# One-core macaron block (MoE, attention, MoE): the down products alternate between two PSUM banks, and the attention's products share the two that are left

## What is computed

```python
x = x + 0.5 * ffn(layernorm(x))          # first pass  (a = 0)
x = x + attention(layernorm(x))
x = x + 0.5 * ffn(layernorm(x))          # second pass (a = 1), the same weights

def ffn(x):                               # 2048 tokens of width 256, 8 experts of width 512
    w = top_p_weights(softmax(x @ router_w.T), 0.9)
    for e in range(8):
        out += (silu(x @ gate_w[e].T) * (x @ up_w[e].T)) @ down_w[e].T * w[:, e:e + 1]

def attention(x):                         # 8 sequences of 256; 16 query heads, 4 KV heads, width 16
    q, k, v = rope(rms_norm(x @ Wq.T + bq)), rope(rms_norm(x @ Wk.T + bk)), x @ Wv.T + bv
    return softmax(causal(q @ k.T / 4)) @ v @ Wo.T + bo
```

## Time and profile before

| what | value |
|---|---|
| three runs | 1108.98 us median, 1108.06 to 1111.28 |
| the profiled execution | 1108.69 us, span of the core 1107.0 us |
| PE matmuls busy | 1087.7 us, 98% of the span |
| DVE / ACT / POOL busy | 853.8 / 546.2 / 641.0 us |
| mean granted TensorE clock | 0.996 |

### The profile page before, as it was taken

One profiled execution on the slowest core, in us unless ns is written; L12 is line 12 of the kernel. 1 busy time (PEld: TensorE's weight loads), 2 busy tenths in 40 slices (PEclk: granted clock), 3 DMA queues, 4 the chain that ended last, 5 costly groups with the idle time before them and its releaser, 6 DMA issues.

```text
span 1107.0 us, 21233 instructions
## 1 busy us (share of the span) xinstructions
PE 1087.7 (98%) x7624; PEld 657.0 (59%) x7624; DVE 853.8 (77%) x1810; ACT 546.2 (49%) x1027; POOL 641.0 (58%) x673
## 2 busy tenths in 40 slices
PE   6899999999999999999999999999999999999998
PEld 4466656565665655566566566656656566666655
DVE  7988788767878887889888789888888765644443
ACT  4545554333555655645655555555555553333332
POOL 4545343346668677778677678586686643322332
PEclk8999999999999999999999999999999999999999
DMA  5311120010133333323333523443243320000000
GB/s 191 127 58 57 58 82 1 1 25 20 35 67 63 61 60 68 58 49 67 65 56 53 86 41 61 74 84 61 49 68 59 78 57 6 6 20 1 1 1 20
DMA packets 166008, 57.96 MB, mean 52 GB/s; under 512 B 158096, under 2 KB 162704, under 8 KB 165904
## 3 DMA queue, kind: packets, MB, share of 16 engines
q1 hardware_dynamic: 165904, 56.61, 24.7%
HBM read 15.70 MB, written 2.10 MB: 16 GB/s over the span
## 4 chain that ended last, share of the span: by engine, by line
PE 79%; DVE 3%; POOL 3%; issue 1%; DMA 1%; ACT 0%; DVEq 0%; ACTq 0%; POOLq 0%; SPq 0%
PE YB L358 25%; PE G L339 25%; PE U L339 24%; PE S L448 2%; PE S L431 1%; PE S L413 1%; PE S L459 1%; POOL room L1090 1%; POOL HS L1006 1%; DMA QKT<-room 1%; DVE TS L625 0%; DVE X L646 0%; ACT TS L500 0%; POOL RR L1063 0%; PE S L358 0%
## 5 line engine op out<-in xcount | busy, mean ns | idle before, releaser
L1006 POOL TENSOR_TENSOR HS<-TS,HS 128x512 f16<-128x512 f32 x256 | 300.7, 1176 | 394.8 <-ACT HS L507 394.1
L358 PE MATMUL YB<-W,HS 128*128 128x256 f16 x3036 | 373.4, 273 | 7.0 <-DVE X L646 4.6
L339 PE MATMUL G<-XS,W 128*128 128x512 f16 x1536 | 374.7, 380 | 0.3 <-ACT XS L533 0.3
L339 PE MATMUL U<-XS,W 128*128 128x512 f16 x1536 | 373.5, 379 | 0.0
L358 PEld LDWEIGHTS YB<-W,HS 128*128 128x128 f16 x3036 | 292.0, 98 | 89.4 <-DVE X L646 8.8
L507 ACT ACTIVATE HS<-TS 128x512 f16<-128x512 f32 x256 | 161.0, 629 | 320.5 <-DVE TS L630 319.3
L625 DVE SCALAR_TENSOR_TENSOR TS<-TS,G 128x512 f32<-128x512 f32 x256 | 174.8, 683 | 136.8 <-ACT TS L500 134.9
L500 ACT ACTIVATE TS<-G,TSC 128x512 f32<-128x512 f32 x256 | 175.1, 684 | 189.6 <-PE G L339 186.5
L339 PEld LDWEIGHTS U<-XS,W 128*128 128x128 f16 x1536 | 150.4, 98 | 181.7 <-issue 0.8
L339 PEld LDWEIGHTS G<-XS,W 128*128 128x128 f16 x1536 | 146.2, 98 | 131.9 <-issue 4.1
L630 DVE SCALAR_TENSOR_TENSOR TS<-TS,U 128x512 f32<-128x512 f32 x256 | 175.9, 687 | 27.8 <-DVE TS L625 0.5
(11 more groups left out here) (168 smaller groups left out, 759.1 us busy)
## 6 DMA issues: line engine op xcount, KB each, us to landing
room<-in_gate SPq DMA_DIRECT2D x4, 512.0 KB, 4.0
room<-in_up SPq DMA_DIRECT2D x4, 512.0 KB, 4.0
room<-in_down SPq DMA_DIRECT2D x4, 512.0 KB, 3.9
QKT<-in_gate SPq DMA_DIRECT2D x4, 512.0 KB, 4.8
QKT<-in_up SPq DMA_DIRECT2D x4, 512.0 KB, 4.0
QKT<-in_down SPq DMA_DIRECT2D x4, 512.0 KB, 4.7
out_y<-X SPq DMA_DIRECT2D x16, 128.0 KB, 1.8
X<-in_x SPq DMA_DIRECT2D x3, 512.0 KB, 6.9
```

The costliest lines, as they stand in the source:

```text
L339: mm = eng.matmul(bank[:, :], W[:, e, wl, jj, kk * I + m * P:kk * I + (m + 1) * P], flat(XS16[:, b % 2, xl, kk, :, :], 'cq'), start=q == 0 ...
L358: mm = eng.matmul(out, HS[:, j % 2, hl, kk, m * P:(m + 1) * P], W[:, e, wl, 2, kk * D:(kk + 1) * D], start=kk + hl + wl == 0, stop=kk == K ...
L1006: eng.tensor_tensor(HS[:, j % 2, 1, m, :], TS[:, k % 3, :], HS[:, j % 2, 0, m, :], ALU.subtract).then_inc(L['g_lo'].sem, 1)
```

## The change

Down products with odd `k` from `Y2` = 9 on go to `S2`, the others stay in `YB`, so `pe_y(k)` waits for the reading of `k-2` in place of `k-1`. PV moves to `S0`, and Q/K/V, projection and all logits to `S1`; `s2_read` goes, and its waits are split between `s0_read` and `s1_read`, which the scores ask too. The tables of slots are written anew, and the start of the lists of PE, ACT, DVE and POOL is reordered.

```diff
+Y2 = 9
-ROUND_AT = (2, 8, 13, 19, 27, 32)
+ROUND_AT = (2, 7, 14, 20, 26, 32)
-FTP0 = (0, 1, 2, 2)
+FTP0 = (0, 0, 2, 3)
-EVEN_STEP = {'ma': 1, 'mb': 2, 'ea': 3, 'eb': 3, 'ha': 5, 'hb': 5, 'la': 4, 'lb': 4, 't': 2, 'pv': 8, 'o': 8}
-ODD_STEP = {'ma': 1, 'mb': 2, 'ea': 2, 'eb': 3, 'ha': 2, 'hb': 4, 'la': 3, 'lb': 4, 't': 3, 'pv': 8, 'o': 9}
+EVEN_STEP = {'ma': 1, 'mb': 2, 'ea': 3, 'eb': 4, 'ha': 5, 'hb': 5, 'la': 4, 'lb': 4, 't': 3, 'pv': 10, 'o': 11}
+ODD_STEP = {'ma': 1, 'mb': 2, 'ea': 2, 'eb': 3, 'ha': 3, 'hb': 5, 'la': 3, 'lb': 4, 't': 4, 'pv': 8, 'o': 10}
-W_FIRST = {'mx': 0, 'wt': 3, 'wr': 3, 'wb': 5, 'sc': 5, 'hi': 7, 'lo': 7}
-ATT, QKVP, OUTP = (by_tile(-24, -12), by_tile(-11, 1), by_tile(18, 42))
+W_FIRST = {'mx': 1, 'wt': 3, 'wr': 2, 'wb': 4, 'sc': 5, 'hi': 7, 'lo': 7}
+ATT, QKVP, OUTP = (by_tile(-24, -12), by_tile(-12, 0), by_tile(25, 43))
...
+        def y_bank(k):
+            return S2 if k >= Y2 and k % 2 else YB
+
         def logits(r):
-            return (S1 if r < 3 else S2)[:, 0:BT * 3 * E]
+            return S1[:, 0:BT * 3 * E]
...
         def s0_read(eng, s):
             eng.wait_ge(*L['a_e'].at(before(ROUND, s), 'a'))
+            eng.wait_ge(*L['v_pv'].at(before(AT['pv'], s), 'rd'))
...
         def s1_read(eng, s):
             eng.wait_ge(*L['a_e'].at(before(ROUND, s), 'b'))
-            eng.wait_ge(*L['v_ls'].at(before(ROUTE[:3], s), 'ls'))
+            eng.wait_ge(*L['v_ls'].at(before(ROUTE, s), 'ls'))
+            eng.wait_ge(*L['v_qb'].at(before(QKVP, s), 'qb'))
+            eng.wait_ge(*L['v_op'].at(before(OUTP, s, O_STEP['mm']), 'ad'))
...
             if bank is None:
-                bank = YB
-                eng.wait_ge(*L['v_y'].at(k - 1, 'y'))
+                bank = y_bank(k)
+                eng.wait_ge(*L['v_y'].at(k - 1 if y_bank(k - 1) is bank else k - 2, 'y'))
+                if k == Y2:
+                    eng.wait_ge(*L['a_fc'].at(2 * BT - 1, 'xs'))
...
         def pe_pv(eng, i, s):
             t, j = ROUNDS[i]
-            s2_read(eng, s)
+            s0_read(eng, s)
...
-                    o = S2[:, n * VW:(n + 1) * VW]
+                    o = S0[:, n * VW:(n + 1) * VW]
...
             act_fc(eng, 1)
-            act_w(eng, 0, 0)
             act_fx(eng, 2)
             act_fx(eng, 3)
+            act_fc(eng, 2)
+            act_w(eng, 0, 0)
             act_w(eng, 0, 1)
-            act_fc(eng, 2)
             act_fc(eng, 3)
```

More of the change, by code:

```diff
@@ L310, in s1_read @@
                 eng.wait_ge(*L['v_wq'].at(0, 'cl'))
-        def s2_read(eng, s):
-            eng.wait_ge(*L['v_pv'].at(before(AT['pv'], s), 'rd'))
-            eng.wait_ge(*L['v_qb'].at(before(QKVP, s), 'qb'))
-            eng.wait_ge(*L['v_op'].at(before(OUTP, s, O_STEP['mm']), 'ad'))
-            f = max((f for f in range(1, 2 * BT, 2) if FTP[f] < s), default=-1)
-            eng.wait_ge(*L['a_fc'].at(f, 'xs'))
-            if before(ROUTE, s) >= 3:
-                eng.wait_ge(*L['v_ls'].at(before(ROUTE, s), 'ls'))
         def pe_warm(eng, n):
@@ L383, in pe_lg @@
         def pe_lg(eng, r, s):
-            (s1_read if r < 3 else s2_read)(eng, s)
+            s1_read(eng, s)
             if r == 0:
@@ L393, in pe_ftp @@
         def pe_ftp(eng, f, s):
-            (s2_read if f % 2 else s0_read)(eng, s)
+            if f % 2 == 0:
+                s0_read(eng, s)
             eng.wait_ge(*L['a_fc'].at(f - 2, 'xs'))
@@ L412, in pe_qkv @@
                 for xl, wl in ((0, 0), (0, 1), (1, 0)):
-                    mm = eng.matmul(S2[:, 0:QKVW], XTA[:, xl, kk, :], WQ16[:, wl, kk, :], start=q == 0, stop=q == 5)
+                    mm = eng.matmul(S1[:, 0:QKVW], XTA[:, xl, kk, :], WQ16[:, wl, kk, :], start=q == 0, stop=q == 5)
                     q += 1
@@ L458, in pe_op @@
                 for ol, wl in ((0, 0), (0, 1), (1, 0)):
-                    mm = eng.matmul(S2[:, 0:D], OT16[:, ol, kk, :], WO16[:, wl, kk, :], start=q == 0, stop=q == 5)
+                    mm = eng.matmul(S1[:, 0:D], OT16[:, ol, kk, :], WO16[:, wl, kk, :], start=q == 0, stop=q == 5)
                     q += 1
@@ L643, in dve_y @@
                 eng.wait_ge(*L['v_op'].at(b * BT + m, 'ad'))
-            y = (YB if bank is None else bank)[:, 0:D]
+            y = (y_bank(k) if bank is None else bank)[:, 0:D]
             x = X[:, b * BT + m, :]
@@ L830, in dve_qb @@
                 eng.wait_ge(s_aw, 16 * N_AW)
[L831 removed]
+            eng.scalar_tensor_tensor(QKV[:, :], S1[:, 0:QKVW], QSC[:, 0:1], BQKV[:, :], ALU.mult, ALU.add).then_inc(L['v_qb'].sem, 1)
         def dve_ss(eng, t):
@@ L901, in dve_op @@
             x = X[:, t, :]
-            eng.scalar_tensor_tensor(x, S2[:, 0:D], DSC[:, 0:1], x, ALU.mult, ALU.add).then_inc(L['v_op'].sem, 1)
+            eng.scalar_tensor_tensor(x, S1[:, 0:D], DSC[:, 0:1], x, ALU.mult, ALU.add).then_inc(L['v_op'].sem, 1)
         def dve_constants(eng):
@@ L1284, in _ @@
             eng.tensor_tensor(RSF[:, :], VEF[:, :], MH[:, 0:BT], ALU.pow).then_inc(L['g_frs'].sem, BT)
+            pool_f_xl(eng, 0)
+            pool_f_xl(eng, 1)
+            pool_f_xl(eng, 2)
+            pool_f_xl(eng, 3)
+            eng.wait_ge(*L['v_fep'].at(2 * BT - 1, 'eps'))
+            eng.wait_ge(*L['v_fx'].at(BT - 1, 'xn'))
+            eng.tensor_tensor(RSF[:, :], VEF[:, :], MH[:, 0:BT], ALU.pow).then_inc(L['g_frs'].sem, BT)
             eng.memset(LOW[:, :, :], 1.0).then_inc(s_i1, 1)
```

35 lines of the change are left out of this document (14 added, 21 removed).

## The result

The changed kernel takes 1119.33 us (median of four, 1117.46 to 1121.13) against 1108.52 for the kernel before beside it: ratio 1.0089, 95% interval 1.0076 to 1.0102. It is slower by 10.8 us by the medians, and by 9.9 (8.4 to 11.3) by the ratio. The prediction said 1110.2 and 1104.8 to 1114.2. The profiled execution took 1117.46, the fastest of the four; the gap of its span to that of before is 8.7 us. From the first down product to the end, which leaves the start out, it is 9.3 us (1115.7 - 36.71 = 1079.0 against 1107.0 - 37.31 = 1069.7).

The account below looks back on a forecast made before the run. PE was taken as full, so only waits move: -4.0 (second bank, new slots) + 4.8 (seven PVs) + 0.3 (S1 sharing) + 0.5 (start) = +1.6; row-based 1110.3, stated 1110.2 us, range 1104.8 to 1114.2.

Parts of the forecast that it names:

- What bounds it: PE is busy in 98% of the span; no matmul is removed, so the change only takes or gives idle time.
- Second bank, 2.6: Down-product waits for the one bank at 148.11, 212.51, 261.41 and 396.54 go wholly: 2.6 us gained.
- Rival 4: The second bank gives nothing, its waits moving to the next operation needing late DVE: +2.6, 1112.8 us; 5%.
- 352.46 and 615.50, 1.4: New slots remove a down product's wait for POOL's low part (0.9) and a PV's for transposed P (0.5).
- Seven PVs, 4.8: The last PV of seven sequences, now in S0, waits for the next sequence's round 0 exponentials: 7 x 0.7 = 4.8 us lost.
- Rival 1: Those last PVs don't wait because the half "a" exponentials are in time: 1105.4 us, faster by 0.3%; 17%.
- PVs of rounds 2 to 4: PVs now in S0 have 1.5 us to spare after half "a" of the latest scores: no cost.
- Rival 3: The 24 PVs of rounds 2 to 4 wait too, as DVE's maxima are late: 7.2 us more, 1117; 19%.
- Sharing of S1, 0.3: Three logits in S1, read by DVE just before the next scores, cost 0.1 each: 0.3 us, bounds 0 to 1.2.
- The start, +0.5: First gate product 0.5 earlier, but DVE work 1.55 later with 0.6 covered: first down product 0.5 us later.
- rival 2: DVE's 128x3 operation gets ahead of POOL's at 35 us, shrinking the wait at 51.66: 1108.4 us; 12%.
- up to 1.3: If the new start has PE at full clock for the first six gate matmuls, up to 1.3 us come off.

Follow-up runs that it names:

- e3: The changed kernel with all down products back in one bank, other banks and slots as changed: 1121.9 us, ratio 1.0113.
- e14: Changed kernel with e1, e6, the old start, RB two slots later and the projection's addition before PV's reading, plus the second bank from k = 3: 1111.0 us.
- e1: The changed kernel with round 0's half "a" exponentials one slot earlier on ACT: 1114.0 us, ratio 1.0047.
- e12: Changed kernel with e1, e6, the old start, RB two slots later and the projection's addition before PV's reading, plus POOL's power a slot later: 1116.4 us.
- e15: The changed kernel with POOL's ranking of the routing one slot later, where it stood before the change: 1117.5 us, ratio 1.0080.
- e13: The kernel before with the new start alone, POOL's ranking left in its old slot: 1109.7 us, ratio 1.0009.
- e6: The changed kernel with the routing of two batches (exponentials, sums, ranks, weights) twelve slots later: 1116.9 us, ratio 1.0067.
- e4: The kernel before with the new start, and also POOL's ranking a slot earlier: 1112.2 us, ratio 1.0027.
- e16: Changed kernel with e1, e6, the old start, RB two slots later and the projection's addition before PV's reading, plus POOL's ranking a slot later: 1113.2 us.
- e10: Changed kernel with e1, e6 and the old start, plus the rotation's product RB of Q and K two slots later on DVE: 1110.6 us, ratio 1.0019.

## Why the prediction was wrong, step by step

- **What bounds it.** Right: PE full, matmuls unchanged, only waits move.
- **Second bank, 2.6.** Right in size (e3: 2.6), wrong in kind. "They go wholly and don't return in a smaller form" failed at two of four places. The value came from lateness that the change itself made. Rival 4 had the mechanism, that waits move to the next operation that needs the late engine, and e14 shows it in full. The sentence of the Trainium skill (TensorE: Matmul & The Clock Gate, HAM oscillation — how this bites in real kernels) that double-buffering PSUM gave no further gain is about one thin-M kernel. Here 2.6 and 3.7 us were measured, 0.2 and 0.3% of the time, and nothing at the place at 52 us (e14).
- **352.46 and 615.50, 1.4.** Both waits are gone. But the PV ahead of the first now waits 0.97 (350.08). "Q/K/V and all that hangs on them stand one slot earlier" misread the tables: `Q_STEP` changed too, so RB and RA keep their slots, POOL's power is two slots earlier and the high parts are one later.
- **Seven PVs, 4.8.** Right in place, releaser and size: 4.7 by the rows of the kernel after, 4.4 to 5.3 by e1. The size had some luck: 0.63 of wait was read where 0.52 came, and 0.06 was added in place of the 0.15 that the prediction adds to every other wait. With that 0.15 it would have been 7 x 0.84 = 5.9. Rival 1 is out.
- **PVs of rounds 2 to 4, "I cost them at nothing".** The cover of 1.5 us was gone at two of 24 places, by 1.0 each: 2.35. Rival 3 had the cause right and the count wrong.
- **Sharing of S1, 0.3.** The step that failed most. Only the logits were looked at, with a bound of 1.2. The projection shares S1 with the scores too, and three scores waited 1.33, 1.33 and 0.60 for its addition: 3.7 us. "Their readers come one slot after them and the next scores at least two slots after" counts slots. It doesn't say how late DVE is within them. The three logits cost nothing in the kernel after (their scores, at 531.48, 692.34 and 853.19, have no wait), but the bound of 0.4 each was no bound: in e12 they cost 1.66 each.
- **What was not a term at all:** the routing's and Q/K/V's new slots on DVE and POOL. The ranking alone, one slot, is 1.0 to 1.9 (e15), the low parts are 2.25, the transpose at 148.73 is 0.65. The prediction took new slots only as gains. It had the mechanism in its hands: it read that DVE stood still for POOL's whole operation at 35 us, and did not ask where else the two would now meet.
- **The start, +0.5.** Right, in size and in its parts: in e13's profile the first gate product is 0.54 earlier (0.5 was said), the transpose waits 0.77 for the late maximum (1.55 - 0.6 = 0.95), and the first down product is 0.50 later. The first down product started at 36.71 to 39.02 in eight profiles with the new start and 36.72 to 37.76 in eleven with the old one. Their means are 37.9 and 37.35, a difference of 0.5. POOL went ahead of DVE as forecast, at 34.32 against 34.81 in the kernel after; rival 2 is out. The full clock that might come with the new start, "up to 1.3", came in the profile of after: its first down product, at 36.71, is 1.1 ahead of e13's. In most of the other profiles it did not.

So the step that failed is the cover of DVE's readers: the sharing of S1 at 0.3, the PVs of rounds 2 to 4 at nothing, and no term for what the new slots do to DVE. In its place the runs show 8.95 us of waits for a late DVE, directly or through ACT, and a late POOL. For the scores at 548.66 and 709.52, e15 and e6 show that the routing's slots make them late. For the PVs and most low parts no run isolates the cause.

The total is then 9.3 from the first down product on and 0.5 for the start, 9.8. The medians say 10.8 and the ratio 9.9 (8.4 to 11.3), so what is left is within the noise. The gap of 8.7 between the two spans is smaller because the profiled execution of after had PE at full clock from 16 us on; its mean granted clock was 0.998, and that of the other three 0.994 and 0.995.

## What to carry to other kernels

When a bank gets a new pair of users, list every pair of writer and last reader in it, not only the one that seems close, and place the reader in its engine's queue by time, with what stands ahead of it, not by slot number. A second buffer takes away only a part of a wait on a late engine and moves the rest to the next instruction that needs the same engine (1.75 became 1.33, and 2.08 became 1.99). When DVE's and POOL's operations change slots, ask which of them will now run side by side: in the kernel after, e4, e12 and e16 alike, late places have stretched DVE operations ahead of them. Read a small step beside its own reference, not against the median of another group: e10's agreement was no more than that. And when an experiment isolates "one part" of a change, check that its edit has nothing else in it: one number in e4 hid the cause until e13.
